# A graph network on one Trainium2 core: the zeros under the spread queries move from the node stage to the load phase

## The reference

```python
h = jnp.maximum(_layernorm(x, axis=-1), 0.0)
# inside _L0_gnn_ref: k, q, v are one typed 64x64 projection each of every node
ke, qe, ve = (k[src], q[dst], v[src])
kw = typed_head_linear(ke, rel_att, etype)
qw = typed_head_linear(qe, rel_att, etype)
a = (kw * qw).sum(-1) * rel_pri[:, etype].T / sqrt_d
...
h = jax.ops.segment_sum(m * alpha[:, :, None], dst, num_segments=n)
```

## Time and profile before

| | us |
|---|---|
| median of three runs | 13014.88 (13014.31 to 13016.5) |
| the profiled execution, its own time | 13030.92 |
| its span in the trace | 13029.2 |
| load phase, to VectorE's wait at L333 over | 0 to 67.96 |
| load phase, the rest | 67.96 to 86.26 |
| node stage up to the first scatter | 86.26 to 532.79 |
| scatters and the end of the stage | 532.79 to 666.4 |

### The profile page before, as it was taken

One profiled execution on the slowest core, in us unless ns is written; L12 is line 12 of the kernel. 1 busy time (PEld: TensorE's weight loads), 2 busy tenths in 40 slices (PEclk: granted clock), 3 DMA queues, 4 the chain that ended last, 5 costly groups with the idle time before them and its releaser, 6 DMA issues. The chain is left out here.

```text
span 13029.2 us, 52526 instructions
## 1 busy us (share of the span) xinstructions
PE 1855.4 (14%) x8713; PEld 1409.7 (11%) x8713; DVE 5592.5 (43%) x18040; ACT 820.2 (6%) x2734; POOL 8292.4 (64%) x8630
## 2 busy tenths in 40 slices
PE   5500000031000000299400000040000022000004
PEld 4300000031000000266300000030000021000003
DVE  7656666652566565488623223212222221222221
ACT  2200000011000000144200000000000000000000
POOL 0277777756777776400177777657777775777775
PEclk9755555555555555699755555555555555555555
DMA  5533333314333332100022222211221211221221
GB/s 191 171 97 105 104 106 105 105 40 56 110 110 101 110 110 81 13 0 0 17 68 65 64 68 64 60 41 49 54 54 50 54 42 44 54 54 50 54 54 37
DMA packets 457203, 917.11 MB, mean 70 GB/s; under 512 B 253408, under 2 KB 269410, under 8 KB 430862
## 3 DMA queue, kind: packets, MB, share of 16 engines
q0 software_dynamic: 275776, 385.29, 13.4%
q10 hardware_dynamic: 25208, 330.11, 6.2%
q1 hardware_dynamic: 155990, 199.74, 5.6%
HBM read 455.59 MB, written 458.97 MB: 70 GB/s over the span
## 5 line engine op out<-in xcount | busy, mean ns | idle before, releaser
L782 POOL DMA_INDIRECT arena<-tab,src x6256 | 5916.9, 946 | 3139.4 <-issue 1906.3
L1746 DVE TENSOR_TENSOR_SCAN arena<-ce_keep,arena 128x46 f32<-128x46 f32 x6528 | 1343.2, 290 | 3042.5 <-DMA arena<-tab,src 3042.5
L782 POOL DMA_INDIRECT arena<-tab,spread x1564 | 1545.9, 988 | 476.9 <-issue 476.9
L1613 PE MATMUL po<-arena 128*128 128x294 f32 x3128 | 832.5, 429 | 391.9 <-ACT arena L1599 391.9
L958 PE MATMUL c_t<-ident,arena 128*64 128x128 f32 (+1 forms) x3 | 1.2, 400 | 6081.1 <-PEq L1900 6081.1
L1742 DVE TENSOR_TENSOR_SCAN arena<-ce_keep,arena 128x46 f32<-128x46 f32 x544 | 114.8, 291 | 1413.6 <-DMA arena<-tab,src 1413.6
L1613 PEld LDWEIGHTS po<-arena 128*128 128x128 f32 x3128 | 618.9, 199 | 605.2 <-issue 432.4
L958 PEld LDWEIGHTS c_t<-ident,arena 128*64 128x64 f32 (+1 forms) x3 | 0.4, 136 | 6081.9 <-issue 6081.9
L987 PE MATMUL e_t<-ident,arena 128*68 128x128 f32 (+1 forms) x2 | 0.8, 396 | 4285.4 <-PEq L1900 4285.4
L1599 ACT ACTIVATE arena<-arena 128x98 f32<-128x98 bf16 x1564 | 425.2, 364 | 628.2 <-DVE arena L1580 628.2
L987 PEld LDWEIGHTS e_t<-ident,arena 128*68 128x68 f32 (+1 forms) x2 | 0.3, 134 | 4285.9 <-issue 4285.9
(11 more groups left out here) (287 smaller groups left out, 4708.4 us busy)
## 6 DMA issues: line engine op xcount, KB each, us to landing
rows<-arena ACTq DMA_DIRECT2D x34, 3013.0 KB, 10.0
arena<-tab,src POOLq DMA_INDIRECT x6256, 2.4
rows3b<-arena ACTq DMA_DIRECT2D x68, 1472.0 KB, 5.3
rows<-arena ACTq DMA_DIRECT2D x34, 1840.0 KB, 8.2
rows<-arena ACTq DMA_DIRECT2D x34, 1656.0 KB, 5.9
tab<-arena SPq DMA_DIRECT2D x98, 512.0 KB, 2.6
q_start<-arena SPq DMA_DIRECT2D x68, 736.0 KB, 6.0
arena<-q_start SPq DMA_DIRECT2D x34, 1472.0 KB, 6.5
```

Source lines behind the costliest of these rows:

```text
L782: pool.indirect_dma_start(out=rows[b][:, j, :], out_offset=None, in_=table, in_offset=bass.IndirectOffsetOnAxis(ap=idx[:, at:at + 1].bitca ...
L1613: ins = nc.tensor.matmul(ps[b][:, 0:3 * T], hot_lo[b][:, j, :], hot_w[b][:, j, :, :].rearrange("p k t -> p (k t)"), start=(j == 0), stop=( ...
L1746: ins = v.tensor_tensor_scan(out=out[b][:, :, f], data0=keep[:, cols], data1=rin[b][:, :, f], initial=out[1 - b][:, C - 1, f:f + 1], op0=A ...
```

## The change

The 68 stores of zeros to `q_start` leave SP's program in the node stage and are issued by ScalarE in the load phase, behind the nine stores of L301 and ahead of ScalarE's wait for those nine. Their destination rows, their size and their number stay. Their semaphore is now one that lives for the whole kernel (`g.s_blank`); nothing in the load phase waits for it, and GpSimd waits for it where it waited for `s_zero`. The strip of zeros of the load phase moves to arena column 10624 (`BLANK`), a place that nothing overwrites up to there, and VectorE's memset of the node stage (L565) goes. The buffers behind the strip move by 92 columns.

```diff
+BLANK = T * D + -(-T // PAIRS) * NT * D + 2 * (2 * P + P + 2 * 512)
...
+    g.s_blank = ctx.enter_context(nc.semaphore("q_start_zeroed"))
...
-    zeros, at = view(g, at, J)
...
+    zeros, _ = view(g, BLANK, J)
...
                 zero(rows[EP + P:EP + P + 1, :], zeros[0:1, 0:width])
+            q_rows = g.q_start[0:EP, :].rearrange("(p c j) f -> p c (j f)", p=P, c=2 * NC)
+            for c in range(2 * NC):
+                act.dma_start(q_rows[:, c, :], zeros[:, 0:C * D // 2]).then_inc(g.s_blank, 16)
             act.wait_ge(s_zero, 16 * n_zero[0])
...
-    zeros, at = view(g, at, C * D // 2)
+    assert at == BLANK
+    at += J
...
-            v.memset(zeros, 0.0).then_inc(s_blank, 1)
             norm_steps(nc, dve, g, sq, s_v, s_root)
...
-            wait(sp, s_blank, 1)
-
             def body(i, n):
 
-                for k in range(4):
-                    sp.dma_start(q_rows[:, sl(i, 4, k, 1), :].rearrange("p a n -> p (a n)"), zeros).then_inc(s_zero, 16)
                 for x in range(n):
...
-            pool.wait_ge(s_zero, 16 * 2 * NC)
+            pool.wait_ge(g.s_blank, 16 * 2 * NC)
```

More of the change, by code:

```diff
@@ L236, in load_phase @@
     wraw, at = view(g, at, 2, D)
+    assert at <= BLANK
     nin = [0]
@@ L506, in attention_nodes_phase @@
     sem = lambda n: new_sem(nc, ctx, "an_" + n)
-    s_v, s_root, s_hm, s_tr, s_ht, s_kv, s_kvc, s_q, s_tab, s_tca, s_qdone, s_zero, s_blank = map(sem, (
+    s_v, s_root, s_hm, s_tr, s_ht, s_kv, s_kvc, s_q, s_tab, s_tca, s_qdone = map(sem, (
         "v", "root", "masked", "turned", "turned_copied", "kv", "kv_copied", "q_copied", "tab", "tab_copied",
-        "q_stored", "zeroed", "blank"))
+        "q_stored"))
     s_hot, s_cnt, s_pe, s_const, s_start, s_look, s_d = map(sem, (
@@ L545, in attention_nodes_phase @@
     tab = g.tab0.rearrange("(t p e) c -> t p (e c)", p=P, e=ET)
-    q_rows = g.q_start[0:EP, :].rearrange("(p c j) f -> p c (j f)", p=P, c=2 * NC)
     with ExitStack() as inner:
```

## The result

| | before | changed |
|---|---|---|
| median of the runs | 13014.59 us (4 runs, 13012.05 to 13016.5) | 13096.99 us (4 runs, 13094.2 to 13099.07) |
| profiled execution | 13030.92 us | 13094.2 us |
| ratio to before | | 1.0063, 95% interval 1.0046 to 1.0081 |

A forecast was written before the change was run, and what follows sets the result against it. Transfers were taken to bound the load phase and VectorE's work the node stage. 13014.9 us, plus 74.5 for later loads, less 1.2 for the memset, gave 13088 us, range 13046 to 13121.

The forecast's parts named there:

- the nearest rivals: Load phase: VectorE starts at 100 us if only small loads pay, or 172 if all zeros go first; chances 0.13, 0.15.
- The node stage gives nothing: Node stage: taking 68 stores from SP's rounds saves nothing, since no one on VectorE's path waits for them.
- -1.2 us for the memset: Start of the node stage: VectorE's memset is on the path, so removing it saves 1.2 us.
- One packet for one packet: Load phase: SP's and ScalarE's queues alternate by packet; 470.3 turns of zeros at 0.207 us, 97.2 us; chance 0.60.
- all zeros go first: Rival, load phase: a turn of zeros is a whole store, VectorE starts at 171.7 us, total 13117 us; chance 0.15.
- only a part of the loads pays: Rival, load phase: only small loads or only x take turns with zeros, total 13046 or 13054 us; chance 0.13.
- 516 packets to an engine "if spread evenly": Load phase: SP's 8253 load packets divided over 16 DMA engines, giving the number of turns shared with zeros.
- The loads' own 34.6 us: Load phase: full DMA time of SP's loads without zeros, summed from busy shares; a 34.6 us term.
- ScalarE's issues cost 0 to 3 us: End of the load phase: ScalarE's last store issue, by 165 us, is hidden or costs up to 3 us; taken as 0.
- Nothing later gives it back: Phases behind the load phase: each starts when the one ahead ends, so the loads' delay of 74.5 us stays.
- The 0.207 us for a packet of zeros: Load phase: time per packet of zeros, from stores of 1.86 us with 9 packets to an engine; multiplies 470.3 turns.

The follow-up runs named there:

- strip_kept: Changed kernel with all 68 stores back in SP's node-stage rounds, four a round, and VectorE's memset still gone: 13014.39 us, 0.9998 of before.
- types_split: Changed kernel with the node types load of 97 partitions cut into one of 96 and one of 1: 13077.02 us, 1.0051 of before.
- behind_loads: Changed kernel with the 68 stores of zeros on SP's queue behind all the loads instead of on ScalarE's: 13101.44 us, 1.0068 of before.
- weights_on_act_split: strip_kept with 47 weight and small-table loads moved to ScalarE's queue and node types loaded as 96 partitions and 1: 12992.74 us, 0.9981 of before.

## Why the prediction was right, point by point

The time, 13097, is inside the range (13046 to 13121), on the side that was forecast, and 9 us above the 13088. VectorE starts at 153.4 where the forecast had 142.5 and the nearest rivals 100 and 172; x's two loads take SP 53 us where it had some 60; the DMA share of the node stage is 0.32 for 0.33.

**The node stage gives nothing.** Right. 445.48 us with the stores, 445.03 without (strip_kept against the changed kernel). ScalarE, GpSimd and the buffers that moved cost nothing that shows.

**-1.2 us for the memset.** The stage is 1.5 us shorter (1.05 in strip_kept). Too small for the totals.

**One packet for one packet.** Right, and shown twice: 1969 to 1970 packets in 30 us, and the loads 58 us earlier when the zeros come in quarters. The forecast had VectorE at 172 if all zeros go first. That time was too late: the zeros were to be through at 170.3 us, but from 153.4 us on only 193 of their packets are left, and from 156.5 on 16. Part of the difference is x's own time, below; the rest I have not worked out. So VectorE's 153.4 alone is hardly against that rival. What is against it are the counts, and VectorE's 133.0 once the load on one engine is out of the way. That only a part of the loads pays falls by the counts too: x does (30 to 60 us) and the small loads do (84 to 139). Of the rule of the Trainium skill ("DMA: Bandwidth & Descriptors", "Queues, rings and completion order") these runs bear out the round of turns. What a turn holds they show in the profile's packets: one for one in the counts, and on the engine with the node types, where the packets stand singly, one packet of a load for each packet of zeros, not for a whole store of nine.

**516 packets to an engine "if spread evenly".** This is the step that failed. They were not: 97 of them, the node types, sat on one engine. It is worth 20.4 us (types_split). I had the row of that load in the timeline and divided by 16 all the same. That 97 partitions stay on one engine and 96 and 1 do not is what types_split shows; how other counts fall on the engines it does not show.

**The loads' own 34.6 us.** Too high beside stores. Before, from 28 to 38 us, x's packets take 110.1% of 10 us on 16 engines over 2114, 83 ns each; beside the zeros, 18.9% of 30 us over 1970, 46 ns. 194 packets an engine make that 7 us less. So 142.5 - 7 - 1 (zeros at 0.2045 us for 0.207) + 20.4 = 155, for 153.4 measured. Two terms were off, 20 up and 8 down, and by luck the forecast came out nearer than it had earned.

```profile
q1 hardware_dynamic: 2114, 2.16, 110.1%
```

**ScalarE's issues cost 0 to 3 us.** Right for this kernel, 0: they end at 138.8 (the forecast had 165), ahead of VectorE's own end of phase. But the reason was thin. x's load with its thousands of packets in SP's queue is no measure of it: in behind_loads SP is held for 107 of 126 us, so a queue holds some ten stores; in the changed kernel they land 20.1 us behind their issue at the median, which is 11 times 1.86. As the only cost it would have been larger than the one that I forecast: +90.5 us.

```profile
DMA to landing us min/median/max: 15.9/20.1/26.5
```

**Nothing later gives it back.** Right: 85.4 us at the node stage's start, 83.9 at its first scatter, 82.4 in the medians.

## What to carry over

A phase whose DMA engines idle because one sequencer issues small loads has room for other small packets, not for large ones: in these runs two busy queues alternated by packet, so count the packets of the transfer that you wait for, on its fullest engine, and multiply by the length of the neighbour's. An engine that issues more than its queue holds is itself held until it is through, and a barrier behind it waits. Before moving traffic out of a stage, see whether anyone there waits for it: 51 MB of stores cost at most about half a microsecond beside 440 us of VectorE's work when they were spread over it, and 76 us when they were put ahead of it.

## What was not expected of the hardware

- A load of 97 partitions of 512 B ran on one DMA engine. Beside short packets that is hardly seen (2.2 us); beside packets of 5888 B it is 20.4 us and makes what stands behind it on that queue late.
- A packet of x takes 83 ns in the trace alone, 46 ns in turns with stores of zeros, and 82 ns in turns with loads of weights (weights_on_act_split, 28 to 36 us: 97.2% of 8 us on 16 engines over 1513 packets). Why it is shorter beside stores is not shown.
- Stores in pieces of 1472 B ran at 351 GB/s. In pieces of 5888 B they ran at 424 GB/s on the same queue (types_split) and at 414 GB/s on SP's (behind_loads, 80 to 90 us: 4.14 MB).
- The 0.207 us for a packet of zeros is a mean of eight packets of 5888 B, 0.225 to 0.23 us each, and one of 4 B.
- The median gather on GpSimd takes 944 to 947 ns by execution. Over 7820 of them 3 ns move the whole time by 0.2%, as much as small changes do. A single pair of profiled executions can mislead by that.
